# 64-row tiles for the attention products, a centring matrix for the norm, and the inverse roots moved from VectorE to GpSimd

## The reference

```python
def attn_layer(x, Wqkv, qs, ksc, Wo):          # 16 heads of 64
    q, k, v = jnp.split(x @ Wqkv, 3, -1)       # x: half of the features shifted by one token
    q = l2norm(q) * qs; k = l2norm(k) * ksc
    q = q * cos * scale + rotate_half(q) * sin * scale
    k = k * cos / scale + rotate_half(k) * sin / scale
    out = local_attention(q, k, v)             # windows of 32, each sees itself and the one before
    return out @ Wo
def ffn_layer(x, g, bln, W1, b1, W2, b2):
    mu = x.mean(-1, keepdims=True)
    var = ((x - mu) ** 2).mean(-1, keepdims=True)
    xn = (x - mu) / jnp.sqrt(var + 1e-05) * g + bln
    a, gate = jnp.split(xn @ W1 + b1, 2, -1)
    return a * jax.nn.gelu(gate, approximate=False) @ W2 + b2
for i in range(6):
    x = attn_layer(shift_tokens(x), ...) + x
    x = ffn_layer(shift_tokens(x), ...) + x
```

## Time and profile before

| | us |
|---|---|
| median of three runs | 1988.04 |
| the profiled execution, its whole time | 1988.08 |
| its span, first to last instruction | 1986.3 |
| PE, DVE, ACT, POOL busy | 1820.3, 1725.2, 1478.1, 1293.8 |

### The profile page before, as it was taken

One profiled execution on the slowest core, in us unless ns is written; L12 is line 12 of the kernel. 1 busy time (PEld: TensorE's weight loads), 2 busy tenths in 40 slices (PEclk: granted clock), 3 DMA queues, 4 the chain that ended last, 5 costly groups with the idle time before them and its releaser, 6 DMA issues. The chain is left out here.

```text
span 1986.3 us, 58980 instructions
## 1 busy us (share of the span) xinstructions
PE 1820.3 (92%) x21168; PEld 1383.2 (70%) x21168; DVE 1725.2 (87%) x3888; ACT 1478.1 (74%) x2647; POOL 1293.8 (65%) x724
## 2 busy tenths in 40 slices
PE   3947999999999999999999999999999999999984
PEld 2524777777677777677777677777677777677774
DVE  5779889889889889889889889888889888989975
ACT  3335787788787788788788788788788788788772
POOL 2538667667667667667667667667667667667651
PEclk7868999999999999999999999999999999999996
DMA  3001321222321222321222321222321222221220
GB/s 126 1 0 43 97 61 46 63 63 55 103 61 46 62 63 57 102 63 44 62 63 58 100 63 45 61 63 60 99 63 45 60 63 61 66 63 47 59 64 22
DMA packets 80673, 121.49 MB, mean 61 GB/s; under 512 B 16776, under 2 KB 29574, under 8 KB 79750
## 3 DMA queue, kind: packets, MB, share of 16 engines
q1 hardware_dynamic: 80646, 121.14, 22.9%
HBM read 19.36 MB, written 1.05 MB: 10 GB/s over the span
## 5 line engine op out<-in xcount | busy, mean ns | idle before, releaser
L1157 POOL TENSOR_TENSOR rot<-rot,root 128x1024 f32<-128x1024 f32 x192 | 365.4, 1903 | 492.6 <-DVE root L1025 492.6
L710 PE MATMUL r<-wqkv,xs 128*128 (+1 forms) x1152 | 527.8, 594 | 4.6 <-ACT xs L861 3.7
L1142 POOL TENSOR_TENSOR rot<-rot,rot_sin 128x1024 f32<-128x1024 f32 x192 | 451.5, 2375 | 0.0
L890 ACT ACTIVATE squares<-r 128x512 f32<-128x512 f32 x384 | 229.1, 597 | 258.6 <-PE r L710 255.1
L710 PEld LDWEIGHTS r<-wqkv,xs 128*128 128x128 f32 x1152 | 204.7, 191 | 193.3 <-issue 186.5
L987 DVE TENSOR_TENSOR rot_sin<-r,table 128x512 f32<-128x512 f32 x384 | 245.4, 680 | 0.0
L982 DVE TENSOR_TENSOR rot<-r,table 128x1024 f32<-128x1024 f32 x192 | 234.1, 1220 | 9.7 <-ACT squares L890 6.2
L1149 POOL TENSOR_TENSOR squares<-squares 128x512 f32<-128x512 f32 x192 | 241.5, 1281 | 0.0
L715 PE MATMUL r<-square,rot 128*128 128x128 f32 x1536 | 205.5, 278 | 39.1 <-DVE rot_sin L987 30.2
L1162 POOL TENSOR_TENSOR sm<-sm,rowmax 128x1024 f32<-128x1024 f32 x96 | 182.7, 1903 | 64.6 <-DVE rowmax L1035 64.6
L874 ACT ACTIVATE kT<-r 64x1024 f32<-64x1024 f32 x192 | 195.7, 1019 | 35.2 <-PE r L715 34.1
(11 more groups left out here) (130 smaller groups left out, 3271.7 us busy)
## 6 DMA issues: line engine op xcount, KB each, us to landing
vwin<-vtok SPq DMA_DIRECT2D x576, 128.0 KB, 2.3
vwin<-vtok SPq DMA_DIRECT2D x384, 64.0 KB, 2.0
wqkv<-in_wqkv SPq DMA_DIRECT2D x6, 1536.0 KB, 6.4
wo<-in_wo SPq DMA_DIRECT2D x6, 512.0 KB, 3.9
w<-in_w SPq DMA_DIRECT2D x6, 341.0 KB, 3.1
x<-in_x SPq DMA_DIRECT2D x4, 256.0 KB, 3.7
rope<-in_rope SPq DMA_DIRECT2D x1, 1024.0 KB
out_x<-y SPq DMA_DIRECT2D x4, 256.0 KB, 2.3
```

The source lines that it names most:

```text
L710: pe.matmul(dst[:, c * 512:(c + 1) * 512], xs1[:, u, 0:P], w.rearrange("p a n -> p (a n)"), start=True, stop=True).then_inc(S[done], 1)
L890: last = act.activation(squares[:, k, c * 512:(c + 1) * 512], src[:, c * 512:(c + 1) * 512], ACT.Square)
L1142: pool.tensor_tensor(r, r, rot_sin[:, k, :, :, :].rearrange("p h a d -> p h (a d)"), ALU.add)\
L1157: pool.tensor_tensor(r, r, bcast(root[:, k * HEADS:(k + 1) * HEADS], 2, DH), ALU.mult)\
```

## The change

1. `score` and `attend` use products of 64 rows: one head each, 32 columns, 64 results wide, twice as many. The two row halves write to different PSUM banks. kT and vwin lose their zero blocks, so that copy_k and carry_k are one instruction each, and the heads stand in another order in the scores (row sums, the v copy and the output projection are arranged for it).
2. The norm: a matrix `center_w` (unit matrix less 1/128) gives x - mean in one product; ACT copies it to SBUF (`xc`, now in two buffers) and squares it from PSUM, both ahead of the pT copy; the variance is one column; gain and bias are an ACT instruction (`ff_affine`) behind copy_k.
3. DVE makes `minus_half` alone (`root_inputs`). The guess and the Newton steps run on POOL at the head of its step, with 1.5 added by an instruction of its own (`three_halves`): 1 + 3 x 4 = 13 instructions.
4. PE and POOL get an instruction that only adds to a semaphore nobody waits for (`score_begun`, `attend_begun`, `roots_begun`) behind the waits of these stages.

```diff
-ROOT_OPS = 3 + 3 * NEWTON
+ROOT_OPS = 1 + 4 * NEWTON
...
-        kT = sb("kT", [P, 2, FT, 2, WIN + P])
-        vtok = sb("vtok", [P, 2, 2, FT, DH])
-        vwin = sb("vwin", [P, NW, 2, FT, DH])
+        kT = sb("kT", [P, 2, FT, WIN + P])
+        vtok = sb("vtok", [P, 2, 2, FT // 2, 2 * DH])
+        vwin = sb("vwin", [P, NW, FT, DH])
...
+                pe.sem_inc(S["score_begun"], 1)
                 for f in range(FT):
-                    for w in range(NW):
-                        rows = slice(WIN * w, WIN * (w + 1))
-                        last = pe.matmul(dst[rows, f * P:(f + 1) * P], qT[:, f, rows],
-                                         kT[:, u, f, :, WIN * w:WIN * (w + 2)], start=True, stop=True)
+                    for s in range(2):
+                        half = slice(DH * s, DH * (s + 1))
+                        at = 512 * s + 2 * WIN * f
+                        for w in range(NW):
+                            rows = slice(WIN * w, WIN * (w + 1))
+                            last = pe.matmul(dst[rows, at:at + 2 * WIN], qT[half, f, rows],
+                                             kT[half, u, f, WIN * w:WIN * (w + 2)], start=True, stop=True)
...
+                for i in range(FT // 2):
+                    for s in range(2):
+                        for e in range(2):
+                            half = slice(2 * WIN * e, 2 * WIN * (e + 1))
+                            at = 512 * e + DH * (2 * i + s)
+                            for w in range(NW):
+                                rows = slice(WIN * w, WIN * (w + 1))
+                                last = pe.matmul(dst[rows, at:at + DH], pT[half, (FT // 2) * s + i, rows],
+                                                 vwin[half, w, 2 * i + s, :], start=True, stop=True)
...
-                pe.matmul(pm[:, 512:512 + P], mean_w, xs2[:, 0:P], start=True, stop=True).then_inc(S["mean_done"], 1)
+                pe.matmul(pm[:, 512:512 + P], center_w[:, :], xs2[:, 0:P], start=True, stop=True)\
+                  .then_inc(S["center_done"], 1)
...
-                pe.matmul(pm[:, 0:P], xcsq[:, :], mean_w, start=True, stop=True)\
+                pe.matmul(pm[:, 0:1], xcsq[:, :], mean_w[:, 0:1], start=True, stop=True)\
...
-                src = src[:, :].rearrange("p (f t) -> p f t", f=FT)
-                for s in range(2):
-                    rows = slice(64 * s, 64 * s + 64)
-                    last = act.activation(kT[rows, u, :, s, WIN:WIN + P], src[rows, :, :], ACT.Copy)
-                last.then_inc(S["kT_copied"], 1)
+                act.activation(kT[:, u, :, WIN:WIN + P], src[:, :].rearrange("p (f t) -> p f t", f=FT), ACT.Copy)\
+                   .then_inc(S["kT_copied"], 1)
...
-            def ff_square(n):
-                act.wait_ge(S["centered"], n + 1)
-                act.activation(xcsq[:, :], xc[:, :], ACT.Square).then_inc(S["xc_squared"], 1)
+            def ff_square(n, u):
+                act.wait_ge(S["center_done"], n + 1)
+                act.activation(xc[:, u, :], pm[:, 512:512 + P], ACT.Copy).then_inc(S["centered"], 1)
+                if not (isinstance(n, int) and n == 0):
+                    act.wait_ge(S["var_done"], n)
+                act.activation(xcsq[:, :], pm[:, 512:512 + P], ACT.Square).then_inc(S["xc_squared"], 1)
+
+            def ff_affine(n):
+                act.wait_ge(S["hatted"], n + 1)
+                layer = n // NB
+                act.activation(xn2[:, :], xhat[:, :], ACT.Identity, scale=cols[:, 0, bass.ds(layer, 1)],
+                               bias=cols[:, 1, bass.ds(layer, 1)]).then_inc(S["xn2_ready"], 1)
...
+            def root_inputs(n):
                 if runs(n + 1):
                     dve.wait_ge(S["q_summed"], n + 2)
                     dve.wait_ge(S["k_summed"], n + 2)
+                    if runs(n):
+                        dve.wait_ge(S["refined"], ROOT_OPS * (n + 1))
                     dve.tensor_scalar(minus_half[:, 0:2 * HEADS], ss[:, :, :].rearrange("p k h -> p (k h)"),
                                       1e-24, -0.5, ALU.max, ALU.mult)\
-                       .then_inc(S["refined"], 1 if runs(n - 2) else 2)
+                       .then_inc(S["halved"], 1 if runs(n - 2) else 2)
...
+            def find_roots(n):
+
+                before = ROOT_OPS * (n + 1)
+                pool.wait_ge(S["halved"], 2 * (n + 2))
+                if runs(n - 3):
+                    pool.wait_ge(S["rstd_spread"], n - 2)
+                pool.sem_inc(S["roots_begun"], 1)
+                pool.tensor_scalar(root[:, :].bitcast(I32), minus_half[:, :].bitcast(I32), -0.5, GUESS,
+                                   ALU.mult, ALU.add).then_inc(S["refined"], 1)
+                for i in range(NEWTON):
+                    pool.wait_ge(S["refined"], before + 1 + 4 * i)
+                    pool.tensor_tensor(root_t[:, :], minus_half[:, :], root[:, :], ALU.mult)\
+                        .then_inc(S["refined"], 1)
...
+                    pool.tensor_tensor(root_t[:, :], root_t[:, :], three_halves[:, :], ALU.add)\
+                        .then_inc(S["refined"], 1)
+                    pool.wait_ge(S["refined"], before + 4 + 4 * i)
+                    pool.tensor_tensor(root[:, :], root_t[:, :], root[:, :], ALU.mult)\
+                        .then_inc(S["refined"], 1)
...
             def step(n, u):
+                if runs(n + 1) or runs(n - 2):
+                    find_roots(n)
                 if runs(n + 1):
                     scale(n + 1, 1 - u, 1, "k_added", "k_scaled")
```

More of the change, by code:

```diff
@@ L658, in _, with heads_of @@
         def _(sp):
+            def heads_of(part):
+                return part.rearrange("p i (s d) -> p (i s) d", s=2)
             def spread_v(n, u):
@@ L733, in attend @@
                 pe.wait_ge(S["v_spread"], SPREADS * (n + 1))
-                for f in range(FT):
-                    for w in range(NW):
-                        rows = slice(WIN * w, WIN * (w + 1))
-                        last = pe.matmul(dst[rows, f * P:(f + 1) * P], pT[:, f, rows], vwin[:, w, :, f, :],
-                                         start=True, stop=True)
+                pe.sem_inc(S["attend_begun"], 1)
+                for i in range(FT // 2):
+                    for s in range(2):
+                        for e in range(2):
+                            half = slice(2 * WIN * e, 2 * WIN * (e + 1))
[4 more added lines that the diff above has]
+                                                 vwin[half, w, 2 * i + s, :], start=True, stop=True)
                 last.then_inc(S["vwin_free"], 1)
@@ L781, in ff_down @@
                 if runs(n + 1):
[L782 removed]
+                    pe.wait_ge(S["halved"], 2 * (n + 5))
                 pe.wait_ge(S["w2_loaded"], 48 * (n // NB + 1))
@@ L870, in copy_k @@
                 act.wait_ge(S["kT_done"], n + 1)
-                src = src[:, :].rearrange("p (f t) -> p f t", f=FT)
-                for s in range(2):
-                    rows = slice(64 * s, 64 * s + 64)
-                    last = act.activation(kT[rows, u, :, s, WIN:WIN + P], src[rows, :, :], ACT.Copy)
-                last.then_inc(S["kT_copied"], 1)
+                act.activation(kT[:, u, :, WIN:WIN + P], src[:, :].rearrange("p (f t) -> p f t", f=FT), ACT.Copy)\
+                   .then_inc(S["kT_copied"], 1)
             def carry_k(n, u):
                 act.wait_ge(S["kT_copied"], n + 1)
-                for s in range(2):
-                    rows = slice(64 * s, 64 * s + 64)
-                    last = act.activation(kT[rows, 1 - u, :, s, 0:WIN], kT[rows, u, :, s, P:P + WIN], ACT.Copy)
-                last.then_inc(S["k_carried"], 1)
+                act.activation(kT[:, 1 - u, :, 0:WIN], kT[:, u, :, P:P + WIN], ACT.Copy).then_inc(S["k_carried"], 1)
             def square(n, k, src, proj, summed, done):
@@ L1008, in find_roots @@
                     dve.tensor_scalar(minus_half[:, 2 * HEADS:ROOTS], pm[:, 0:1], 1e-5, -0.5, ALU.add, ALU.mult)\
-                       .then_inc(S["refined"], 1 if runs(n + 1) else 2)
-                dve.wait_ge(S["refined"], before + 2)
-                if runs(n):
-                    dve.wait_ge(S["q_scaled"], n + 1)
-                if runs(n - 3):
-                    dve.wait_ge(S["rstd_spread"], n - 2)
-                dve.tensor_scalar(root[:, :].bitcast(I32), minus_half[:, :].bitcast(I32), -0.5, GUESS,
-                                  ALU.mult, ALU.add).then_inc(S["refined"], 1)
-                for i in range(NEWTON):
-                    dve.wait_ge(S["refined"], before + 3 + 3 * i)
-                    dve.tensor_tensor(root_t[:, :], minus_half[:, :], root[:, :], ALU.mult)\
-                       .then_inc(S["refined"], 1)
-                    dve.wait_ge(S["refined"], before + 4 + 3 * i)
-                    dve.tensor_tensor(root_t[:, :], root_t[:, :], root[:, :], ALU.mult)\
-                       .then_inc(S["refined"], 1)
-                    dve.wait_ge(S["refined"], before + 5 + 3 * i)
```

(15 more changed lines are left out.)

79 lines of the change are left out of this document (39 added, 40 removed).

## The result

| | median of 4 runs | range | profiled execution (span) |
|---|---|---|---|
| before | 1987.76 us | 1986.83 to 1988.2 | 1988.1 (1986.3) |
| after | 2015.83 us | 2012.67 to 2019.11 | 2016.33 (2014.5) |

The ratio is 1.0142, interval 1.0124 to 1.016: the change makes the kernel slower by 28 us; I had forecast 38 us faster. The page's busy shares, against the earlier trace rows: PE, DVE and ACT all do less, POOL does more.

What follows compares the result with a forecast made beforehand. A chain DVE - PE - ACT bounded the kernel; after the change Ring B would, at 14.15 + 3.90 = 18.05 us a step against 18.46. Sum: 1988 - 37 - 5 + 4 = 1950 us, range 1885 to 2060.

Steps and rivals of the forecast that it cites:

- Ring B: Cycle of a step through POOL's queue, then DVE's table, hid and minus_half: 14.15 us and 13p, said to decide.
- ring A: Cycle of a step from DVE's hid through POOL's roots and ACT's exp to the gates: 13.92 us and 13p.
- p: Start-to-start time of one of POOL's 13 root instructions: 0.257 to 0.303 us by the rows, taken as 0.30.
- the narrow class from 0.325 to 0.34: Case for POOL's root instruction spacing in us between forecast and slower rival, step unchanged; chance 0.06.
- rival 1: POOL's small instructions are dearer, spacing above 0.33 us; at 0.39 the step is 19.22, 2055 us in all; chance 0.33.
- The reaction 0.08: POOL's delay from the end of DVE's minus_half to its first root instruction, claimed 0.08 us.
- the semaphore additions: Added semaphore instructions in the queues, taken as entries beside running work, with no price.
- Removals at nothing: Work taken from DVE, ACT and PE loosens the old ring by 3 us or more, priced at nothing.
- Tiles: 64-row products in score and attend on PE: at best 0.8 us saved in each, at worst the time of now.
- Rival 3: PE's products cost by number, 26 ns per record, 3.4 us for 128: step +2.0, 2170 us; chance 0.06.
- Layer changes -5: At the five layer changes PE's wait for w2 shrinks with more slack: -5 us (0 to -10).
- start and end +4: At the stack's start and end stages run alone and roots of 3.9 instead of 2.3 us lie bare: +4 us.

Runs made afterwards that it cites:

- e6: The changed kernel with DVE's table of the rotary moved behind minus_half: 1967.3 us, ratio 0.9897.
- e13: The changed kernel with POOL's two waits ahead of the seed in swapped order: 1996.1 us, ratio 1.0038.
- e14: The changed kernel with five semaphore additions ahead of POOL's seed instead of one: 2069.1 us, ratio 1.0409.
- e16: The changed kernel with the seed alone back on DVE and no semaphore addition ahead of POOL's Newton instructions: 1971.3 us, ratio 0.9923.
- e5: The changed kernel with six extra identity products on PE while it waits for exp, ahead of the transposes of probs: 2002.4 us, ratio 1.0066.
- e1: The changed kernel with the seed and Newton instructions back on DVE, 64-row tiles and centring matrix kept: 1886.9 us, ratio 0.9491.
- e8: The kernel before with the new norm alone (centring matrix, ACT's affine), 128-row tiles and roots as before: 1998.5 us, ratio 1.0049.
- e11: The changed kernel with seed and two Newton steps on DVE, the third on POOL, table behind DVE's roots: 1874.7 us, ratio 0.9426.
- e2: The kernel before with the roots alone moved to POOL, 128-row tiles and old norm kept: 2134.5 us, ratio 1.0736.

## Why the prediction was wrong, by its own steps

- **"Ring B is the longer by 0.2 and decides."** Right, and by 0.4. Table, second add, hid and minus_half follow each other as described; moving the table (e6) left ring A, and the step was 18.17 against 18.25 by the formula.
- **"p is thus 0.257 to 0.303 ... I take 0.30": the step that failed.** The 13 instructions take 4.33 us, p = 0.333, outside the bounds. The gap of 0.08 was right (0.078); the record is 0.257 us, not 0.223. The 0.223 drew POOL's line through 1024 and 512 numbers down to 33 (done without rounding the two rows give 149 fixed and 0.221, 2 us less in the whole). This moved the step by +0.43 and alone turned -0.41 into nothing. p = 0.333 lies in the narrow class from 0.325 to 0.34, "where the step stays as it is", which I gave 0.06; it isn't rival 1's 0.39. The Trainium skill (GPSIMD Engine Reference, section Performance versus the Vector engine) gives 1.96 times VectorE's time for an add of 2048 numbers. At 33 numbers the trace shows less: 0.257 to 0.195 for the record, 1.3 times, and 0.333 to 0.229 for the chain, 1.45.
- **"The reaction 0.08", and "the semaphore additions ... no price".** Wrong: 0.27 (e13, e14, e16). Against it hid starts 0.08 before the table's record ends, and the other terms come to 0.03 less: ring B without its 13 is 14.23, for 14.15.
- **PE's clock: left out altogether.** I had noted that exp would wait for POOL and that PE would have slack, and took slack for free. Behind PE's wait before the transposes of probs the clock falls in 13 of 77 steps, +15 us (e5). It is the largest part of the 27 us that p leaves (below). This is a term, not a size: no row of before showed 1.2 GHz in a steady step, and I didn't ask what a longer wait would do.
- **Removals at nothing.** Right for the forecast's own ring. What they are worth without it e1 shows: 101 us, a ring at 17.36.
- **Tiles.** 128 records of score take 1.61 us, of attend 1.48, for 1.95 each before: 0.34 and 0.47 saved, between the 0.8 and the nothing of my bounds. Rival 3 (26 ns a record, 3.4 us) is refuted. What I called products there, "four products start within 0.04 us", are records; a float32 product is two of them. The Trainium skill (TensorEngine Tiling, section Instruction Overhead) puts some 60 cycles on each matmul. Here a record starts each 12.6 ns (1.61 / 128), about 30 cycles at 2.4 GHz, but a product as written each 25.2 ns (1.61 / 64), about 60; by products the trace agrees with the page, by records it doesn't, and no run tells which of the two the pace goes by.
- **Layer changes -5, start and end +4.** -8.0 and +13.3: the first six steps, three of them at 1.2 GHz in part where the kernel before has none, cost 8.1.

With p = 0.333 the forecast's own formula gives 18.48 a step and 1989 us, no change. The rest of the way to 2016, 27 us, is the clock 15, start and end 9 more, the ring's other terms 6, less 3 at the layer changes.

## What to carry to other kernels

A short instruction's price on another engine isn't found by drawing the line of its long ones down to zero; where thirteen of them stand in a ring, 0.03 us each is the whole forecast, and a range should then span both signs. Before calling an engine's new slack free, ask what that engine does after a longer wait: TensorE came back at half its clock in 13 of 77 steps. And an instruction that is taken out may have covered another wait: the tiles alone gave 26 us, and 112 once the new norm had removed the wait behind them (e8 to e1). So take a change apart in both directions.

## What the runs showed of the hardware

- GpSimd, chained on its own results at 128 x 33: 0.257 us a record, 0.078 us between; the seed (tensor_scalar) 0.225. Each semaphore addition ahead of an instruction 0.08 us, a second wait's value 0.07 (e13, e14).
- DVE's table, two SBUF operands, doesn't slow down beside POOL's two-operand adds but stops until they end: 1.72 us instead of 0.41, ending 0.28 behind the second add, in all 64 steady steps at 2.4 GHz; just ahead of the 33-number instructions it takes 0.41 (e6), beside them 0.47 (e11). DVE's gain and bias (tensor_scalar, 128 x 128) does the same: 1.80 us in e2 instead of 0.34. The Trainium skill (SBUF — State Buffer, section Terms) says of the port pair shared by the two engines that the loser fully blocks; the trace agrees.
- TensorE was at 1.2 GHz for 3.4 us behind 13 of 35 waits of 1.9 us, in a loop in which it is otherwise busy; with 1.5 us of products without use in that wait (e5) it stayed at 2.4 GHz.
